# An expert's low part subtracted one item later, and two gathers of routing shares issued three scatters apart

## The chip, the cores and the metric

The kernel runs on one core of a Trainium2 chip. The metric is the device time of one execution in microseconds (us); three executions of a kernel are taken and their median is compared.

## What is computed

1024 tokens of 256 features pass through a linear layer with low-rank adapters (the condition), and the result goes through a mixture of 8 experts, of which each token uses the best 2. The output is the input plus the mixture. Cut to what matters here:

```python
router_logits = xf @ w_gate.T                       # xf: 1024 conditioned tokens
routing_weights = softmax_integer(router_logits)    # fixed-point table of exp
top_w, top_i = jax.lax.top_k(routing_weights, 2)
top_w = top_w / top_w.sum(axis=-1, keepdims=True)
combine = jnp.zeros((T, E)).at[jnp.arange(T)[:, None], top_i].add(top_w)
for e in range(8):
    h = jax.nn.silu(xf @ w1[e].T) * (xf @ w3[e].T)  # 256 -> 704
    out = out + combine[:, e:e + 1] * (h @ w2[e].T) # 704 -> 256
return x + out
```

All inputs and outputs are fp32.

## The kernel before, in words

Only the chosen tokens of an expert are computed. The 2048 choices are sorted by expert into 23 **slots** of 128 rows (SLOTS), every slot belonging to one expert; with these inputs the experts receive 263, 261, 263, 262, 206, 267, 249 and 277 choices, so that the slots of experts 0 to 7 are 3, 3, 3, 3, 2, 3, 2 and 3 in number. A slot is worked off in three **items** (STEPS), each a share of the 704 hidden features, so that the main loop has 69 items; item i is step j = i % 3 of slot s = i // 3.

To keep fp32 accuracy with TensorE's faster formats, every operand is split into a high part (a rounded copy) and a low part (the operand less its high part). Each product is then made of three matmuls.

What each engine does for item i, in its own program order:

- **TensorE**: `gate_up(i)` (L1169, L1178) into one of four PSUM banks `gu`; at one step of each slot the turn of the next slot's rows (L1149); `turn_hidden(i - 1)` (L1185), a transpose of the hidden tile; `down(i - 2)` (L1206 to L1208, and L1200 and L1201 for the last of a slot) into the one PSUM bank `ya`. The first `down` of a slot begins the sum in `ya` anew and so waits for `y_out`, that is until the slot before has been copied out.
- **ScalarE**: `silu(i)` (L611, or L615 and L616 at j = 2), the high part of the next slot's rows (`xs_hi`, L553) and the high part of the hidden tile (`h_hi`, L553).
- **VectorE**: `hidden(i)` (L872, or L877 and L879), the low part of the next slot's rows (L864), `hidden_lo(i - 1)` (L887), and at j = 1 `slot_out(s - 1)` (L893), the copy of `ya` into `rows`, which raises `y_out`. Some further work is put at single items: `SHARED_AT` names the items at which `expert_lo(e, 2)` (L847) stands, the low part of the third piece (1280 columns) of the weights of experts 2 and 3. It raises `third_ready`.
- **GpSimd (POOL)**: makes the rest of the low parts (and from expert 4 on the high parts) of the weights and issues the gathers of the slots' rows in between (L452). For expert 3 it waits for `third_ready` before its last step `tail_low` (L463), which raises `w_ready`; TensorE waits for `w_ready` when it is about to begin an expert. After the last expert POOL scatters each finished slot's rows to HBM (L474): `scatter(s)` waits for `hid_done` to reach s + 44 (PACE), so that there is one scatter per item, and for `y_out`.

The last two slots (DIRECT) aren't scattered but joined by matmuls at the end. They need the routing shares of their rows: VectorE works the shares out at items 47 to 52, ScalarE's queue stores them to HBM (L664) at item 53, and two indirect gathers on POOL's queue (L536), one for each slot, fetch 128 numbers of 4 bytes each into `share`. `SHARES_BEHIND` names the scatter after which they are issued. ScalarE waits for both (`share_in`) at item 67, in `direct_hi`. All weights' transfers are issued by SyncE.

The lines that decide the order around the change:

```python
if j == turned_at(s) and s + 1 < SLOTS:
    slot_lo(s + 1)
...
if 1 <= i <= ITEMS:
    hidden_lo(i - 1)
...
if i in SHARED_AT:
    expert_lo(SHARED_AT[i], 2).then_inc(third_ready, 1)
if i >= 4 and j == 1:
    slot_out(s - 1)
```

Of the kernel before, what the change touches and what calls it, by code (L numbers as in the profile page):

```python
# [60 lines left out]
DIRECT = 2  # L61
# [9 lines left out]

CLEAR = SLOTS - HI_COLS // DIM
FETCHED = {2: (CLEAR, 10), 3: (10, 14), 4: (14, 18), 5: (18, 20), 6: (20, 21), 7: (21, SLOTS)}
SHARED_AT = {8: 2, 13: 3}

# [1 line left out]

SHARES_AT = ITEMS - 22  # L80
SHARE_PARTS = 6
SHARES_BEHIND = 12
STAGED = 1
STAGED_LOW = 3

# [19 lines left out]
def moe_kernel(nc, x_dram, pack_dram, idx_dram, w_dram, wtail_dram, comb_dram, out_dram):  # L105
    c_dram = nc.dram_tensor("cond_rows", (TOKENS, DIM), F32, kind="Internal").ap()
    y_dram = nc.dram_tensor("expert_rows", (TOP * TOKENS + SLOTS * P, DIM), F32, kind="Internal").ap()
    share_dram = nc.dram_tensor("shares", (P * TOP * TILES, 1), F32, kind="Internal").ap()
    with ExitStack() as ctx:
        def sb(name, shape, dt=F32):  # L110
            return ctx.enter_context(nc.sbuf_tensor(name, shape, dt))
# [4 lines left out]
        def sem(name):  # L116
            return ctx.enter_context(nc.semaphore(name))
# [49 lines left out]
        share_at = sb("share_at", [P, DIRECT], U32)  # L167
        share = sb("share", [P, DIRECT])
# [136 lines left out]
        share_in = sem("share_in")  # L305
# [110 lines left out]
        def _(pool):  # L416
# [53 lines left out]
            def scatter(s):  # L470
                pool.wait_ge(dst_ready, 1)
                pool.wait_ge(rows_zeroed, 16)
                pool.wait_ge(y_out, s + 1)
                nc.gpsimd.indirect_dma_start(  # L474
                    out=y_dram[:, :], out_offset=bass.IndirectOffsetOnAxis(ap=dst_i[:, s:s + 1], axis=0),
                    in_=rows[:, s, :], in_offset=None).then_inc(scattered, 16)
# [52 lines left out]
            for s in range(SENT):  # L529
                pool.wait_ge(hid_done, s + PACE)  # L530
                scatter(s)
                if s == SHARES_BEHIND:
                    pool.wait_ge(share_at_ready, 1)
                    pool.wait_ge(share_out, 16 * TOP)
                    for l in range(DIRECT):
                        nc.gpsimd.indirect_dma_start(  # L536
                            out=share[:, l:l + 1], out_offset=None, in_=share_dram[:, :],
                            in_offset=bass.IndirectOffsetOnAxis(ap=share_at[:, l:l + 1], axis=0)).then_inc(share_in, 16)

            pool.wait_ge(pool_step, 4)  # L540
            for l in range(DIRECT):
# [134 lines left out]
        def _(dve):  # L676
# [167 lines left out]
            def expert_lo(e, k):  # L844
                cols = PIECES[k]
                dve.wait_ge(whi_ready, len(PIECES) * e + k + 1)
                return nc.vector.tensor_tensor(lo_part(e, cols), from_raw(e)[:, cols], as_f32(hi_part(e, cols)),  # L847
                                               ALU.subtract)
# [9 lines left out]
            def expert_tail_lo(e):  # L858
                stack = stack_part(e, LOW_HALF)
                return nc.vector.tensor_tensor(stack, raw_tail(e, LOW_HALF), as_f32(stack), ALU.subtract)  # L860
# [89 lines left out]
            for i in range(ITEMS + 2):  # L950
# [21 lines left out]
                if i == 3:  # L972
                    destinations()
                    expert_lo(1, 2)
                    expert_tail_lo(1).then_inc(w_ready, 1)
# [3 lines that stand above are left out]
# [355 lines left out]
```

## Time and profile before

| what | value |
|---|---|
| three executions | 203.08, 204.21 and 204.86 us; median 204.21 us |
| the profiled execution | 204.69 us, of which the span from the first to the last instruction is 203.0 us |
| busy share of the span | TensorE 95%, VectorE 54%, ScalarE 41%, GpSimd 64% |
| TensorE's granted clock | full speed (2.4 GHz) throughout |

The profile is one execution of the program, taken by the hardware profiler. Times in its rows are microseconds from the start of the span; "PE" is TensorE's matmuls, "PEld" its weight loads, "DVE" VectorE, "ACT" ScalarE, "POOL" GpSimd. L847 is line 847 of the kernel. The ends of matmuls are modelled, since they are pipelined; spans on POOL are rough.

### The profile page before, as it was taken

Reading aid. Unit: us, or ns where it says so; the run is one execution under the profiler, and the core shown is the slowest. Engines: PE = TensorE matmul, PEld = TensorE weight load, DVE = VectorE, ACT = ScalarE, POOL = GpSimd, SP = SyncE. Lnnn points to the kernel's source line nnn. Section 1 sums busy time; section 2 is a strip of 40 time slices with the busy share of each in tenths; the row PEclk is TensorE's granted clock in tenths of the full one; section 3 lists DMA queues with packets and bytes.
Section 4 is the critical chain, followed back from the end, with each engine's and each line's share of the span. In section 5 each row is a group of like instructions: output and inputs, shape, how many; then the busy total and the mean of one; then the engine's idle time right before and its main releaser. Section 6 shows DMA issues by size and latency. Waiting matters only on the chain.

```text
span 203.0 us, 3879 instructions
## 1 busy us (share of the span) xinstructions
PE 192.1 (95%) x1209; PEld 169.2 (83%) x1209; DVE 108.7 (54%) x308; ACT 82.4 (41%) x224; POOL 129.7 (64%) x116
## 2 busy tenths in 40 slices
PE   7699999899998999999999999999999997999992
PEld 6387997788897899889988998899888886989881
DVE  0678899783646345334534453444675434435483
ACT  2576583368733143323332343233323323333560
POOL 8300004559899999999999999996345473316700
PEclk9999999999999999999999999999999999999999
DMA  5999320799996115283274383017212111110915
GB/s 134 408 368 361 136 103 19 232 301 385 349 396 235 57 55 155 61 284 75 88 258 126 90 260 113 0 16 275 74 55 53 53 55 61 43 55 26 346 73 208
DMA packets 14403, 32.67 MB, mean 161 GB/s; under 512 B 2384, under 2 KB 7632, under 8 KB 14256
## 3 DMA queue, kind: packets, MB, share of 16 engines
q1 hardware_dynamic: 10704, 25.17, 36.2%
q0 software_dynamic: 2128, 5.64, 8.8%
q10 hardware_dynamic: 1552, 1.61, 2.4%
q8 instruction: 12, 0.20, 0.4%
q14 instruction: 7, 0.06, 0.1%
HBM read 25.45 MB, written 6.96 MB: 160 GB/s over the span
## 4 chain that ended last, share of the span: by engine, by line
PE 80%; DVE 10%; DMA 5%; ACT 2%; issue 1%; SPq 0%; DVEq 0%
PE gu L1169 27%; PE gu L1178 14%; PE ya L1206 8%; PE ht L1185 7%; PE ya L1207 7%; PE ya L1208 6%; DMA x<-x_t 4%; DVE w_all L847 3%; PE xt L1149 2%; PE gu L1223 2%; DMA rows<-cond_rows,src_i 2%; PE ya L1201 1%; PE gu L1055 1%; PE ya L1200 1%; PE gu L1236 1%
## 5 line engine op out<-in xcount | busy, mean ns | idle before, releaser
L1169 PE MATMUL gu<-w_all,xs_hi 128*128 (+2 forms) x276 | 70.9, 378 | 0.1
L872 DVE TENSOR_TENSOR hid<-gu,sg 128x256 f32<-128x256 f32 x46 | 19.5, 425 | 65.8 <-ACT sg L611 62.5
L1169 PEld LDWEIGHTS gu<-w_all,xs_hi 128*128 128x128 f32 x276 | 46.8, 188 | 4.4 <-issue 0.3
L611 ACT ACTIVATE sg<-gu 128x256 f32<-128x256 f32 x46 | 17.7, 384 | 75.3 <-PE gu L1178 75.3
L458 POOL TENSOR_TENSOR w_all<-raw,w_all 128x1024 fp32r<-128x1024 f32 (+2 forms) x14 | 44.0, 3156 | 3.6 <-DVE w_all L860 3.5
L452 POOL DMA_INDIRECT rows<-cond_rows,src_i x22 | 23.6, 1073 | 30.5 <-DVE src_i L828 25.9
L1206 PE MATMUL ya<-w_all,h_hi 128*128 (+1 forms) x115 | 38.4, 334 | 2.4 <-DVE rows L893 2.3
L1178 PE MATMUL gu<-w_all,xs_lo 128*128 (+1 forms) x138 | 40.6, 375 | 0.0
L474 POOL DMA_INDIRECT expert_rows<-rows,dst_i x21 | 20.3, 969 | 26.3 <-DVE hid L872 14.5
L1207 PE MATMUL ya<-w_all,h_hi 128*128 (+1 forms) x115 | 32.5, 282 | 0.0
L1208 PE MATMUL ya<-w_all,h_lo 128*128 (+1 forms) x115 | 32.2, 280 | 0.0
L1178 PEld LDWEIGHTS gu<-w_all,xs_lo 128*128 128x128 f32 x138 | 25.6, 188 | 4.0
L887 DVE TENSOR_TENSOR h_lo<-ht,h_hi 128x256 fp32r<-128x256 f32 x69 | 28.6, 415 | 0.3 <-ACT h_hi L553 0.3
L553 ACT ACTIVATE h_hi<-ht 128x256 fp32r<-128x256 f32 x69 | 26.7, 387 | 0.5 <-PE ht L1185 0.4
L1185 PE MATMUL ht<-ident,hid 128*128 128x128 f32 x138 | 26.3, 272 | 0.3 <-DVE hid L872 0.3
L1206 PEld LDWEIGHTS ya<-w_all,h_hi 128*128 128x128 f32 x115 | 21.7, 188 | 4.6 <-issue 3.7
L1185 PEld LDWEIGHTS ht<-ident,hid 128*128 128x128 f32 x138 | 18.5, 140 | 4.7 <-DVE hid L872 0.6
L1207 PEld LDWEIGHTS ya<-w_all,h_hi 128*128 128x128 f32 x115 | 21.8, 190 | 0.0
L1208 PEld LDWEIGHTS ya<-w_all,h_lo 128*128 128x128 f32 x115 | 21.7, 189 | 0.0
L507 POOL CAST w_all<-raw 128x1024 fp32r<-128x1024 f32 (+2 forms) x12 | 16.8, 1401 | 0.0
L615 ACT ACTIVATE sg<-gu 128x128 f32<-128x128 f32 x23 | 6.4, 279 | 21.9 <-PE gu L1178 19.6
L877 DVE TENSOR_TENSOR hid<-gu,sg 128x128 f32<-128x128 f32 x23 | 6.7, 291 | 12.4 <-ACT sg L616 11.7
(190 smaller groups left out, 261.1 us busy)
## 6 DMA issues: line engine op xcount, KB each, us to landing
raw<-expert_weights SPq DMA_DIRECT2D x6, 896.0 KB
raw<-expert_weights SPq DMA_DIRECT2D x6, 640.0 KB
raw<-expert_weights SPq DMA_DIRECT2D x6, 512.0 KB
expert_rows<-zeros SPq DMA_DIRECT2D x1, 2048.0 KB
rows<-expert_rows SPq DMA_DIRECT2D x4, 512.0 KB, 5.0
cond_rows<-c_rows ACTq DMA_DIRECT2D x4, 256.0 KB, 2.0
raw<-x_t SPq DMA_DIRECT2D x1, 1024.0 KB
out_t<-raw SPq DMA_DIRECT2D x4, 256.0 KB, 2.2
```

The costliest lines, as they stand in the source:

```text
L452: nc.gpsimd.indirect_dma_start(out=rows[:, s, :], out_offset=None, in_=c_dram[:, :], in_offset=bass.IndirectOffsetOnAxis(ap=src_i[:, s:s + ...
L458: return nc.gpsimd.tensor_tensor(lo_part(e, cols), from_raw(e)[:, cols], as_f32(hi_part(e, cols)), ALU.subtract)
L474: nc.gpsimd.indirect_dma_start(out=y_dram[:, :], out_offset=bass.IndirectOffsetOnAxis(ap=dst_i[:, s:s + 1], axis=0), in_=rows[:, s, :], in ...
L553: return nc.scalar.activation(out, in_, ACT.Copy)
L872: nc.vector.tensor_tensor(hid[i % HBUFS][:, :].rearrange("p (a b) -> p a b", b=P), bank[:, :].rearrange("p (a k b) -> p a k b", k=2, b=P)[ ...
L887: nc.vector.tensor_tensor(h_lo[i % HBUFS][:, :], ht[i % 2][:, 0:2 * P], as_f32(h_hi[i % HBUFS][:, :]), ALU.subtract).then_inc(h_lo_ready, 1)
L1169: nc.tensor.matmul(out, stay_hi[:, kc * P:(kc + 1) * P], moving(at, part + first + kc * P, n), start=kc == 0 and part == HI_COLS, stop=False)
L1178: last = nc.tensor.matmul(out, stay_lo[:, kc * P:(kc + 1) * P], moving(at, first + kc * P, n), start=False, stop=kc == KC - 1)
L1185: last = nc.tensor.transpose(ht[i % 2][:, q * P:(q + 1) * P], hid[i % HBUFS][:, q * P:(q + 1) * P], ident[:, :])
L1206: nc.tensor.matmul(out, stay_hi, w_l, start=j == q == 0, stop=False)
L1207: nc.tensor.matmul(out, stay_hi, w_h, start=False, stop=False)
L1208: last = nc.tensor.matmul(out, stay_lo, w_h, start=False, stop=False)
```

## The change

`SHARED_AT` moves expert 3's third piece from item 13 to item 14. Item 13 is step j = 1 of slot 4 and has a `slot_out`, ahead of which the subtraction stood; item 14 is step j = 2 and has none. The second of the two gathers of shares, which stood right behind the first after scatter 12, is now issued after scatter 15. The two waits ahead of a gather stand ahead of each of them.

```diff
-SHARED_AT = {8: 2, 13: 3}
+SHARED_AT = {8: 2, 14: 3}
...
-SHARES_BEHIND = 12
+SHARES_BEHIND = (12, 15)
...
                 scatter(s)
-                if s == SHARES_BEHIND:
+                if s in SHARES_BEHIND:
+                    l = SHARES_BEHIND.index(s)
                     pool.wait_ge(share_at_ready, 1)
                     pool.wait_ge(share_out, 16 * TOP)
-                    for l in range(DIRECT):
-                        nc.gpsimd.indirect_dma_start(
-                            out=share[:, l:l + 1], out_offset=None, in_=share_dram[:, :],
-                            in_offset=bass.IndirectOffsetOnAxis(ap=share_at[:, l:l + 1], axis=0)).then_inc(share_in, 16)
+                    nc.gpsimd.indirect_dma_start(
+                        out=share[:, l:l + 1], out_offset=None, in_=share_dram[:, :],
+                        in_offset=bass.IndirectOffsetOnAxis(ap=share_at[:, l:l + 1], axis=0)).then_inc(share_in, 16)
```

## Rows read from the trace of the kernel before

**Rows 1.** The page, busy time: us, share of the span, instructions.
```profile
PE 192.1 (95%) x1209; PEld 169.2 (83%) x1209; DVE 108.7 (54%) x308; ACT 82.4 (41%) x224; POOL 129.7 (64%) x116
```

**Rows 2.** The chain that ended last: start, us, what.
```profile
64.32 1.40 DVE w_all L847
...
94.63 0.94 PE gu L1169 x4
...
166.41 1.95 PE gu L1178 x2
```

**Rows 3.** Busy time by stretch, slots 3 and 4, cut at each slot's first matmul.
```profile
core 0: us, PE busy (x) PEld busy (x) DVE busy (x) ACT busy (x) POOL busy (x), PEclk, DMA share, GB/s
52.23:59.03 6.80, 6.80 (x45) 6.12 (x44) 4.72 (x13) 3.75 (x11) 6.31 (x5) 1.00 1.12 368
59.03:67.28 8.25, 7.04 (x44) 6.16 (x44) 4.58 (x11) 2.26 (x8) 7.46 (x5) 1.00 0.64 243
```

**Rows 4.** The same view, slots 18 and 19.
```profile
156.33:163.14 6.81, 6.81 (x45) 6.04 (x44) 2.92 (x10) 2.27 (x8) 3.56 (x4) 1.00 0.21 60
163.14:171.43 8.29, 7.23 (x45) 6.10 (x44) 3.17 (x10) 2.26 (x8) 4.76 (x6) 1.00 0.15 50
```

**Rows 5.** All waits of PE: who waited, us in total, times, longest.
```profile
PE ya L1206 <- DVE rows L893: 2.3, 3, 1.2
```

**Rows 6.** Timeline, items 13 and 14: start, us, engine, line; idle time before it.
```profile
62.83 0.38 PE L1185 MATMUL ht<-ident,hid 128*128 128x128 f32 x2
...
64.23 1.48 DVE L847 TENSOR_TENSOR w_all<-raw_low,w_all 128x1280 fp32r<-128x1280 f32 x1
...
64.71 0.38 PE L1185 MATMUL ht<-ident,hid 128*128 128x128 f32 x2
64.83 1.71 POOL L452 DMA_INDIRECT rows<-cond_rows,src_i  x1 [0.30 <-issue]
...
65.63 0.42 DVE L893 COPY rows<-ya 128x256 f32<-128x256 f32 x1
...
66.30 0.38 PE L1206 MATMUL ya<-w_all,h_hi 128*128 x1 [1.21 <-DVE rows L893]
...
67.81 0.75 POOL L463 TENSOR_TENSOR w_all<-raw_low_tail,w_all 64x256 fp32r<-64x256 f32 x1
```

**Rows 7.** Timeline of DVE, items 8 and 9, then 11 and 12.
```profile
52.74 1.48 DVE L847 TENSOR_TENSOR w_all<-raw,w_all 128x1280 fp32r<-128x1280 f32 x1
54.42 0.42 DVE L872 TENSOR_TENSOR hid<-gu,sg 128x256 f32<-128x256 f32 x1 [0.19 <-ACT sg L611]
...
58.89 0.41 DVE L887 TENSOR_TENSOR h_lo<-ht,h_hi 128x256 fp32r<-128x256 f32 x1
60.91 0.42 DVE L872 TENSOR_TENSOR hid<-gu,sg 128x256 f32<-128x256 f32 x1 [1.60 <-ACT sg L611]
```

**Rows 8.** Timeline of POOL from 134 to 172 us.
```profile
140.51 0.96 POOL L474 DMA_INDIRECT expert_rows<-rows,dst_i  x1 [0.34 <-issue]
...
162.47 0.98 POOL L536 DMA_INDIRECT share<-shares,share_at  x1 [0.30 <-issue]
163.75 0.96 POOL L536 DMA_INDIRECT share<-shares,share_at  x1 [0.30 <-issue]
...
166.33 0.98 POOL L474 DMA_INDIRECT expert_rows<-rows,dst_i  x1 [0.31 <-issue]
```

**Rows 9.** Timeline of all engines around item 58.
```profile
160.08 0.38 ACT L611 ACTIVATE sg<-gu 128x256 f32<-128x256 f32 x1 [1.67 <-PE gu L1178]
...
166.25 0.62 PE L1178 MATMUL gu<-w_all,xs_lo 128*128 x2
...
168.38 0.38 ACT L611 ACTIVATE sg<-gu 128x256 f32<-128x256 f32 x1 [2.99 <-PE gu L1178]
```

**Rows 10.** DMA queues, packets: the stretch 158.75 to 159.0, then 166 to 168 us.
```profile
q14 instruction: 1, 0.01, 12.6%
...
q0 software_dynamic: 85, 0.18, 26.1%
```

## The prediction

> **What bounds the kernel now.** I read the page's busy times first: TensorE is busy 95% of the span and VectorE 54% [rows 1], so TensorE sets the end, and a change elsewhere is worth only what TensorE stands idle for it. Next the chain that ended last. It consists of matmuls from item to item, and two places break the pattern: a VectorE piece of 1.40 us at 64.32, which is the subtraction of expert 3's third piece, and a pair of L1178 matmuls credited with 1.95 us at 166.41 [rows 2], where the timeline gives the two matmuls 0.62 [rows 9]. Then the busy times cut at each slot's first matmul: an ordinary slot takes 6.80 or 6.81 us, slot 4 takes 8.25 and slot 19 takes 8.29 [rows 3, 4]. So TensorE loses 1.45 us in one slot and 1.48 us in another. The clock was full in all four stretches. The list of TensorE's waits names VectorE's copy L893 as the greatest releaser, 2.3 us in three waits, the longest 1.2 [rows 5]; the only row of it that names POOL is of a memset at the start, so no weights were late.
>
> The timeline shows the first loss. In item 14 TensorE turned the hidden tile at 64.71 and could have begun the next slot's `down`, but `ya` was not copied out: VectorE had begun the subtraction at 64.23, took 1.48 us, and copied at 65.63; TensorE went on at 66.30 [rows 6]. The second loss starts on another engine: the matmuls of item 58 ended at 166.25 + 0.62 = 166.87, and ScalarE's silu, idle and waiting for nothing else in its program, began only at 168.38, after 2.99 us of idleness where the same step a slot earlier had 1.67 [rows 9]. VectorE's chain and the copy of `ya` came late behind it. What held ScalarE is named nowhere. What lies just ahead are the kernel's only two gathers of 4-byte shares, issued at 162.47 and 163.75, with late scatters behind them [rows 8].
>
> **Part 1: the subtraction an item later.** It takes away the 1.48 us ahead of the copy. The copy then follows the low part of the hidden tile at about 64.23 and ends near 64.65, about when the transposes at 64.71 are issued [rows 6], so the wait goes. The gain is the whole excess of the slot, 8.25 - 6.80 = 1.45 us [rows 3]; the named wait of 1.21 us [rows 6] is the lower bound. I take 1.45, since that is what TensorE's schedule lost.
>
> The same instruction is put back at item 14. There VectorE ends an ordinary j = 2 item with the low part at 58.89 + 0.41 = 59.30 and starts the next product at 60.91, after 1.60 us of idleness [rows 7]; 1.48 us fits with 0.12 to spare. Expert 2's third piece is a precedent at the same step: it started at 52.74 in item 8, took 1.48 us, and the next product still waited 0.19 us for ScalarE [rows 7]; the stretch in which it lies took TensorE 6.80 us [rows 3]. If the cover were gone, the product would be late by the excess, and TensorE turns such a tile at 62.83, that is 1.50 us after the product's end at 60.91 + 0.42 = 61.33 [rows 6, 7]; only what goes beyond that costs. Cost: zero, at most 0.1 us.
>
> POOL waits for this piece ahead of `tail_low`. With the stall gone, slot 5 begins at 59.03 + 6.80 = 65.83, the low part ends some 0.27 us behind that as it did a slot earlier, at 66.1, and the piece ends at about 67.6; POOL reaches `tail_low` at 67.81 today [rows 3, 6, 7]. So it comes just in time; half a microsecond late would do no harm either, since expert 3 begins with slot 9 (the first three experts fill three slots each), whose matmuls start at 94.63 [rows 2]. Behind `tail_low` on POOL stands the conversion of expert 4, needed later still. The gather of rows that lay beside the piece took 1.71 us [rows 6] where the like gathers of scattered rows take 0.96 [rows 8]: the later piece will stretch the next gather instead, and its rows are not wanted for slots.
>
> The piece itself took 1.48 us with a gather beside it and without change from one place to the other [rows 6, 7], so VectorE was not held up by POOL. The Trainium skill (SBUF — State Buffer, "SBUF: two separate sides") says that a VectorE operation with two SBUF inputs and a GpSimd operation that reads SBUF exclude each other, and that whichever starts first keeps the shared ports to its end. By that rule a POOL operation that started first would delay the piece by up to its own length, and with the 0.96 us of a gather the next product would be 0.8 us late, inside the 1.50 us of cover; the sum would be the same by row and by rule.
>
> **Part 2: the gathers apart.** No instruction is added: the two waits ahead of the second gather (the shares stored, their addresses made) were over before the first. Scatter 13 comes 1.28 us earlier (163.75 - 162.47), scatter 16 waits that long behind the second gather; a scatter is released each item, that is each 6.80 / 3 = 2.3 us, so the backlog is gone after one. Scatter 15 is three items behind scatter 12, one slot: with part 1's gain taken off, the first gather goes out at 162.47 - 1.45 = 161.0 and the second 6.8 us later, at 167.8. ScalarE needs it in item 67, nine items or three slots (20 us) after item 58. On these counts the cost is zero. The gain is bounded by the stall: at most 8.29 - 6.81 = 1.48 us [rows 4], at least zero, and below zero if each gather alone brings such a stall, +1.48. I take 1.48: this is the one place where ScalarE is late in the steady loop, and it follows the one pair of gathers. Indirect transfers in quick succession alone don't do it: the scatter at 140.51 was the last of four about 1.3 us apart [rows 8], and the chain shows nothing late there.
>
> **The sum.** 204.69 - 1.45 - 1.48 = 201.76, say 201.8 us. The profiled execution is 0.48 above the median of 204.21; on the median the same sum gives 201.28. The lowest execution, 203.08, is 1.61 below the profiled one, about one stall; so the second loss may not be there in every execution, and then 203.08 - 1.45 = 201.63 is what all would come to. What is late next: nothing as large; the rest of the loop runs at 6.8 us a slot, and the end shifts with it.
>
> **Rivals.**
> *The ScalarE stall stays, once.* Its cause is not shown. If it belongs to the first gather, or to ScalarE's own program at that point, only part 1 counts: 204.69 - 1.45 = 203.24 us, 202.8 on the median. For it: nothing in the trace ties ScalarE to a gather. Against: the place. In the stretch of the stall only the software queue of the gathers and scatters carried packets, 85 of them; the nearest packet of the small instruction queue lies at 158.75 [rows 10], eight microseconds earlier. The Trainium skill (Runtime: NRT & Kernel Launch, "Instruction fetch mechanics") says that each engine fetches its program in blocks through a queue of its own, mostly hidden. By that rule a stall at a block's border would stay with its instruction and give the time of this rival; the trace has no such packet in the stall.
> *Each gather brings its own stall.* Scatter 15 is released by an item of the same step as scatter 12's, one slot later, so the second gather meets ScalarE in the same phase as the first. If each alone holds ScalarE for 1.48 us, two slots lose what one loses now: 204.69 - 1.45 + 1.48 = 204.72 us, slower than before by a trace, by 0.5 us against the median. It decides as soon as one gather's stall exceeds 1.45 us. Against: two gathers 1.28 us apart show one stall today.
> *The subtraction stalls TensorE again.* Were the piece stretched beyond 0.12 + 1.50 us, or the copy of `ya` late for another reason, the first gain is lost and the second stays: 204.69 - 1.48 = 203.21 us.
> *Neither gain comes:* 204.7 us.
>
> **How the numbers follow.** Forecast 0.50; the stall stays 0.30; two stalls 0.08; the first gain lost 0.07; neither 0.05. The forecast's own range is 201.0 to 202.2 (201.28 on the median less 0.3, 201.8 and 0.4 for the spread of executions). With the rivals at 202.8 to 203.24 and 0.4 for the spread, 201.0 to 203.7 holds the time 8 times in 10. One per cent, about what a measurement of this kernel tells from no change, is 2.04 us: faster means below 202.17, slower above 206.25. Faster is the forecast but for its upper edge, 0.44, and 0.03 of the second case: 0.47. Slower is 0.03, the rest 0.50.
>
> **What would show it.** Right: slot 4 at 6.8 us; the copy L893 ahead of L847, and L847 ending before the next product; the longest wait for L893 gone from TensorE's list; POOL's `tail_low` near 67.8; gathers near 161.0 and 167.8; all slots from 16 to 21 at 6.8 to 7.0 us, and no silu later than 0.1 us behind its matmuls. Wrong: a slot of over 8 us behind one gather or both, or a new idle stretch ahead of the product of item 15. The prediction fails if the ScalarE stall is not the gathers' doing.

## The result and the profile after

The changed kernel takes 202.97 us (median of 7 executions, 202.05 to 203.54), the kernel before, run beside it, 204.21 us (7, 203.08 to 204.99). The ratio is 0.9933, 95% interval 0.9905 to 0.996: a gain of 0.7%, less than the one per cent that the prediction counts as faster. The profiled execution of the changed kernel took 203.51 us, with a span of 201.8 us, 1.2 us less than before. The forecast was 201.8, its range 201.0 to 203.7; the time is that of the rival "the ScalarE stall stays, once" (202.8 on the median). Why it came out there is another matter.

Busy times of the changed kernel, cut as [rows 3] and [rows 4] are: slots 3, 4, 18 and 19; then two stretches near the start.

```profile
core 0: us, PE busy (x) PEld busy (x) DVE busy (x) ACT busy (x) POOL busy (x), PEclk, DMA share, GB/s
53.80:60.62 6.82, 6.82 (x45) 6.13 (x44) 4.74 (x13) 3.82 (x11) 5.48 (x6) 1.00 1.10 366
60.62:67.47 6.85, 6.85 (x45) 6.15 (x44) 3.01 (x10) 2.27 (x8) 6.08 (x4) 1.00 0.68 262
...
156.68:163.49 6.81, 6.81 (x44) 6.13 (x44) 2.85 (x10) 2.26 (x8) 3.56 (x4) 1.00 0.21 60
163.49:170.30 6.81, 6.81 (x44) 6.12 (x44) 3.00 (x10) 2.27 (x8) 3.87 (x5) 1.00 0.18 60
...
8.00:10.00 2.00, 1.91 (x7) 1.47 (x8) 1.48 (x6) 0.88 (x2) 0.00 (x0) 0.66 1.06 440
10.00:12.00 2.00, 2.00 (x8) 1.78 (x7) 1.65 (x2) 1.61 (x5) 0.00 (x0) 0.50 0.99 414
```

Both long slots are gone: slot 4 takes 6.85 us where it took 8.25 [rows 3], slot 19 takes 6.81 where it took 8.29 [rows 4]. That is 2.88 us, close to the forecast's 1.45 + 1.48, yet the span fell by only 1.2. The last two lines say where most of the rest went: between 8 and 10 us TensorE was granted 0.66 of its clock in the mean, and between 10 and 12 us 0.50, that is the lower of its two levels, 1.2 GHz. The same stretches of the profile of before had the full clock, 2.4 GHz:

```profile
8.00:10.00 2.00, 1.59 (x10) 1.04 (x8) 1.68 (x6) 0.95 (x1) 0.00 (x0) 1.00 1.03 430
10.00:12.00 2.00, 1.84 (x12) 1.66 (x13) 1.80 (x2) 2.00 (x5) 0.00 (x0) 1.00 0.99 412
```

Set silu beside silu, the two traces differ so. The first silu of the loop starts 1.13 us later in the changed kernel (33.79 against 32.66 us): the clock. At item 6 it is 1.59 later: ScalarE's copy of a piece of weights waited 1.92 us for the piece to land, where before it waited 1.45. At item 15 it is 0.20 later: 1.40 us came back in slot 4. At item 60 it is 1.17 earlier: 1.35 came back in slot 19. So +1.13 + 0.46 - 1.40 - 1.35 = -1.16, which leaves 0.01 of the 1.17 to small shifts in between. Neither of the first two is touched by the change, which begins at item 13. A single pair of profiles could not tell what the change did.

The step of part 1, timeline of the changed kernel, items 13 to 15 (start, us, engine, line, tiles; in brackets the idle time before it and who ended it):

```profile
65.83 0.42 DVE L893 COPY rows<-ya 128x256 f32<-128x256 f32 x1
...
66.49 0.38 PE L1206 MATMUL ya<-w_all,h_hi 128*128 x1
67.06 0.95 POOL L452 DMA_INDIRECT rows<-cond_rows,src_i  x1 [0.30 <-issue]
67.66 1.48 DVE L847 TENSOR_TENSOR w_all<-raw_low,w_all 128x1280 fp32r<-128x1280 f32 x1
69.29 0.73 POOL L463 TENSOR_TENSOR w_all<-raw_low_tail,w_all 64x256 fp32r<-64x256 f32 x1 [1.28 <-DVE w_all L847]
69.32 0.42 DVE L872 TENSOR_TENSOR hid<-gu,sg 128x256 f32<-128x256 f32 x1 [0.18 <-ACT sg L611]
```

The copy now stands ahead of the subtraction, `down` begins at 66.49 without the 1.21 us of waiting of [rows 6], and the subtraction ends at 69.14, before the product at 69.32. In the list of TensorE's waits the longest for that copy is 0.3 us in place of 1.2 [rows 5]:

```profile
PE ya L1206 <- DVE rows L893: 0.3, 1, 0.3
```

Around item 58, POOL's gathers of shares and ScalarE's silus of items 58 and 60 in the changed kernel:

```profile
162.80 0.98 POOL L536 DMA_INDIRECT share<-shares,share_at  x1 [0.30 <-issue]
167.24 0.38 ACT L611 ACTIVATE sg<-gu 128x256 f32<-128x256 f32 x1 [1.67 <-PE gu L1178]
169.62 0.97 POOL L536 DMA_INDIRECT share<-shares,share_at  x1 [0.31 <-issue]
171.72 0.38 ACT L611 ACTIVATE sg<-gu 128x256 f32<-128x256 f32 x1 [1.72 <-PE gu L1178]
```

The gathers stand 6.82 us apart, and no silu is late: 1.67 us of idleness where [rows 9] had 2.99. The profile looks as the forecast wanted it. Whether the gathers had anything to do with it had to be tried.

### The profile page after: what moved, and what is told of

Read it like the earlier page. It is cut to its first block, busy times and chain, and to the rows that moved or that the text cites. A ratio compares the mean times of both kernels' runs of the same rounds, so it can differ in the third digit from the quotient of the medians.

```text
span 201.8 us, 3880 instructions
## 1 busy us (share of the span) xinstructions
PE 193.5 (96%) x1209; PEld 170.7 (85%) x1209; DVE 108.6 (54%) x308; ACT 82.5 (41%) x224; POOL 127.7 (63%) x116
## 3 DMA queue, kind: packets, MB, share of 16 engines
q10 hardware_dynamic: 1552, 1.61, 2.5%
## 4 chain that ended last, share of the span: by engine, by line
PE 83%; DVE 8%; DMA 5%; ACT 1%; issue 1%; DVEq 0%; SPq 0%
PE gu L1169 27%; PE gu L1178 14%; PE ya L1206 8%; PE ht L1185 7%; PE ya L1207 7%; PE ya L1208 7%; DMA x<-x_t 3%; PE xt L1149 2%; DVE w_all L847 2%; PE gu L1223 2%; DMA rows<-cond_rows,src_i 2%; PE ya L1201 1%; PE ya L1200 1%; PE gu L1055 1%; PE gu L1236 1%
## 5 line engine op out<-in xcount | busy, mean ns | idle before, releaser
L452 POOL DMA_INDIRECT rows<-cond_rows,src_i x22 | 21.9, 994 | 31.6 <-DVE src_i L828 27.1
```

The lines of the kernel that those rows point to most:

```text
L452: nc.gpsimd.indirect_dma_start(out=rows[:, s, :], out_offset=None, in_=c_dram[:, :], in_offset=bass.IndirectOffsetOnAxis(ap=src_i[:, s:s + ...
```

## The experiments

Theory A, the prediction's: the subtraction and the pair of gathers each cost about 1.45 us in every execution. Theory B, its rival: part 1 alone brings the gain, and the late silu belongs to something else, chance included. The lines above leave both open.

**Each part alone.** e1 is the kernel before with part 1 only, e2 with part 2 only.

```diff
-SHARED_AT = {8: 2, 13: 3}
+SHARED_AT = {8: 2, 14: 3}
```


> Part 1 alone: the third piece of expert 3 at item 14, both gathers behind scatter 12 as before. Theory A (the two gathers in quick succession hold ScalarE for 1.5 us in most executions): slot 4 takes 6.8 us, but a silu some 3 to 5 us behind the second gather begins 1.3 to 1.5 us late; the median is about 1.4 us above that of the changed kernel, 204.2 to 204.4 us. Theory B (the late silu is a rare event that the gathers don't cause, so that part 1 is the whole gain): no late silu behind the gathers, and the median is that of the changed kernel, 203.0 us, ratio to before 0.993.

```diff
-SHARES_BEHIND = 12
+SHARES_BEHIND = (12, 15)
...
-                    for l in range(DIRECT):
-                        nc.gpsimd.indirect_dma_start(
+                    nc.gpsimd.indirect_dma_start(
```


> Part 2 alone: the second gather behind scatter 15, the third piece at item 13 as before. Slot 4 keeps its 8.25 us under every theory. Theory A: no late silu, the median 1.4 us under before, ratio 0.993, 202.8 us. Theory B: the median is that of before, ratio 1.000 within 0.003, 204.2 us.

Measured: e1 203.07 us (12 executions), ratio 0.9945 (0.9919 to 0.9971), a gain of 1.12 us (0.59 to 1.66) against 204.45. e2 203.86 us (12), ratio 0.9987 (0.9960 to 1.0015), a gain of 0.27 us (-0.31 to 0.82). The interval of e2 leaves out 1.48 us. In e1's profile no silu is late, though its two gathers follow each other as before; the gathers and the silu of item 58 in e1:

```profile
161.25 0.98 POOL L536 DMA_INDIRECT share<-shares,share_at  x1 [0.30 <-issue]
162.53 0.96 POOL L536 DMA_INDIRECT share<-shares,share_at  x1 [0.30 <-issue]
165.70 0.39 ACT L611 ACTIVATE sg<-gu 128x256 f32<-128x256 f32 x1 [1.67 <-PE gu L1178]
```

So A's second half, a cost in every execution, falls.

**The pair elsewhere, and more pairs.** e3 keeps the gathers together and moves them four scatters on, with part 1. If the pair held ScalarE, the late silu would move with it. e4 adds to part 1 four further pairs behind scatters 13 to 16, into a tile that nothing reads (work added, none left out); SyncE waits for them at the end.

```diff
-SHARES_BEHIND = 12
+SHARES_BEHIND = 16
```


> Part 1 with the pair of gathers, still back to back, four scatters later (behind scatter 16). Theory A: the late silu goes with the pair, to some 3 to 5 us behind 171 to 173 us, and costs 1.3 to 1.5 us there (less if it falls on a step with more slack); about 204.3 us. Theory B: no late silu tied to the pair, 203.0 us. If the late silu stays at item 58, it belongs to ScalarE's own program.

```diff
+MORE = (13, 14, 15, 16)
...
+                if s in MORE:
+                    for l in range(DIRECT):
+                        at = MORE.index(s) * DIRECT + l
+                        nc.gpsimd.indirect_dma_start(
+                            out=share_more[:, at:at + 1], out_offset=None, in_=share_dram[:, :],
...
+            sp.wait_ge(more_in, 16 * DIRECT * len(MORE))
```


> Part 1 with the pair behind scatter 12 and the same two gathers repeated, into a scratch tile, behind scatters 13 to 16: five pairs, ten gathers. Theory A: up to five late silus of 1.5 us each, a median 3 to 7 us above the kernel with one pair. Theory C (each gather costs on its own): the same or more. Theory B: POOL's backlog of scatters grows by some 8 us and is gone before the last scatter; no late silu, 203.0 us.

Measured: e3 202.85 us (10), ratio 0.9923 (0.9891 to 0.9955). e4 203.69 us (10), ratio 0.9985 (0.9956 to 1.0013), about 0.6 us above e1's median; among executions of like clock it is 1.25 us (below). Timeline of e4, the last added pair and the silu behind it (its lines stand ten lower):

```profile
172.73 0.96 POOL L546 DMA_INDIRECT share_more<-shares,share_at  x1 [0.30 <-issue]
173.99 0.94 POOL L546 DMA_INDIRECT share_more<-shares,share_at  x1 [0.30 <-issue]
177.07 0.39 ACT L621 ACTIVATE sg<-gu 128x256 f32<-128x256 f32 x1 [1.75 <-PE gu L1188]
```

Five pairs, and no silu is late behind one; in e3 none either, with the pair at 170.78 and 172.07. What e4's profile lost against e1's, 0.9 us, lies at the end: from its last silu to the end of the span 13.21 us where e1 has 12.33. POOL is later with its own last steps, since eight gathers at 1.26 us stand ahead of them, and TensorE's last stage waits for POOL:

```profile
PE gu L1233 <- POOL w_all L552: 0.4, 1, 0.4
```

Each of these programs has one profile, so a stall that the pairs bring in few executions would not show; five in every execution, 3 us or more, are ruled out by the times.

**The kernel before again.** If the late silu belongs to the program, it comes in each execution. Three more profiles of the kernel before, unchanged.

> The kernel before once more, for its profile: does the late silu of item 58 come again? Theory A (the two gathers bring it): yes, in most looks, at the item 3 to 5 us behind the second gather. Theory B (an event by chance, not tied to the gathers): in few looks or none, or at another item; the other slots 6.8 us, slot 4 at 8.25 us each time.

> As the first look. Theory A: the late silu again. Theory B: not, or elsewhere; slot 4 at 8.25 us.

> As the first look. Theory A: the late silu again. Theory B: not, or elsewhere; slot 4 at 8.25 us.

Measured: 204.70, 203.82 and 203.60 us. Busy times of the first of them, slots 4 and 19:

```profile
60.49:68.74 8.25, 7.04 (x44) 6.16 (x44) 4.59 (x11) 2.27 (x8) 7.46 (x5) 1.00 0.63 234
...
164.63:171.44 6.81, 6.81 (x44) 6.17 (x44) 2.98 (x10) 2.27 (x8) 4.17 (x5) 1.00 0.18 60
```

Slot 4 is as long as in [rows 3], slot 19 is an ordinary slot. The silu of item 15 comes 3.81, 3.82 and 3.82 us after that of item 14 in the three, 3.80 in the first profile, 2.40 in e1. No silu is late in any of the three. Of all 14 profiles of this study one has it, the very one that the prediction was made from; of the 12 whose gathers follow each other, one.

**What part 1 rests on.** e5 leaves the subtraction at item 13 and only swaps the two `if` blocks, so that the copy comes first: if the order alone is the cure, the later item isn't needed.

```diff
-                if i in SHARED_AT:
-                    expert_lo(SHARED_AT[i], 2).then_inc(third_ready, 1)
                 if i >= 4 and j == 1:
                     slot_out(s - 1)
+                if i in SHARED_AT:
+                    expert_lo(SHARED_AT[i], 2).then_inc(third_ready, 1)
```


> Only the order is changed: the third piece stays at item 13 but stands behind the copy of the slot's rows; the gathers as before. Theory of part 1 (the cost is the wait of TensorE for the copy, not the subtraction): the copy starts 1.4 us earlier and slot 4 takes 6.8 us. The product of item 14, whose VectorE idle time is 0.68 us in ordinary slots, comes some 0.7 us late, but TensorE needs it 1.3 us after its ordinary end, so that nothing is lost: ratio 0.993, 203.1 us. Rival (VectorE's room in an item decides, and an item of step 1 has too little): slot 4 keeps 0.5 to 0.8 us of its excess, ratio 0.997.

e6 and e7 load item 14 further, with part 1: one and two subtractions of 1024 columns into space that is free there, ahead of the piece (work added, none left out). They measure the cover that the prediction counted as 0.12 us of idleness and 1.50 us until TensorE turns the tile.

```diff
+                if i == 14:
+                    spare_out = hot_r[:, :, :].rearrange("p a b -> p (a b)").bitcast(F32)
+                    for _ in range(1):
+                        chain(nc.vector.tensor_tensor(spare_out, raw_low[:, DOWN_AT:DOWN_AT + HALF * 2],
...
```


> Part 1 with one extra subtraction of 1024 columns (some 1.2 us, written to a tile that nothing reads any more) ahead of the third piece at item 14. If the cover is as the prediction said (0.12 us of VectorE's idle time and then TensorE's 1.3 to 1.5 us before it needs the late product and low part), the product of item 15 is late by 1.1 to 1.2 us and TensorE loses nothing: slot 5 begins on time and the median is that of part 1, 203.1 us. If VectorE's 1.60 us are the whole cover, TensorE loses 1.1 us and the median is 204.2 us.

> The same with two extra subtractions: 3.9 us of work against 1.60 us of idle time, the product late by 2.3 to 2.4 us. With the further cover of 1.3 to 1.5 us TensorE loses 0.8 to 1.1 us (204.0 us); without it 2.3 us (205.4 us).

Measured: e5 202.30 us (7), ratio 0.9914 (0.9883 to 0.9946). e6 202.27 us (9), ratio 0.9904 (0.9878 to 0.993). e7 203.72 us (10), ratio 0.9973 (0.9944 to 1.0001). Timeline of e5:

```profile
64.15 0.41 DVE L893 COPY rows<-ya 128x256 f32<-128x256 f32 x1
64.48 1.48 DVE L847 TENSOR_TENSOR w_all<-raw_low,w_all 128x1280 fp32r<-128x1280 f32 x1
64.71 2.08 POOL L452 DMA_INDIRECT rows<-cond_rows,src_i  x1 [0.30 <-issue]
65.89 0.28 DVE L877 TENSOR_TENSOR hid<-gu,sg 128x128 f32<-128x128 f32 x1
67.03 0.38 PE L1185 MATMUL ht<-ident,hid 128*128 128x128 f32 x2
```

The next product stands right behind the piece and TensorE turns it on time. Timeline of e7:

```profile
66.22 2.53 DVE L979 TENSOR_TENSOR hot_r<-raw_low,w_all 128x1024 f32<-128x1024 f32 x2
68.79 1.49 DVE L847 TENSOR_TENSOR w_all<-raw_low,w_all 128x1280 fp32r<-128x1280 f32 x1
70.20 0.42 DVE L872 TENSOR_TENSOR hid<-gu,sg 128x256 f32<-128x256 f32 x1
70.67 0.44 PE L1191 MATMUL ht<-ident,hid 128*128 128x128 f32 x2 [0.71 <-DVE hid L872]
71.09 0.38 PE L1212 MATMUL ya<-w_all,h_hi 128*128 x1
```

The same product, turn and `down` of item 15 in e1:

```profile
67.89 0.43 DVE L872 TENSOR_TENSOR hid<-gu,sg 128x256 f32<-128x256 f32 x1 [0.17 <-ACT sg L611]
69.80 0.38 PE L1185 MATMUL ht<-ident,hid 128*128 128x128 f32 x2
69.94 0.36 PE L1206 MATMUL ya<-w_all,h_hi 128*128 x1
```

In e6 the added 1.27 us make the product 1.15 us late (69.04 against 67.89 in e1, 0.09 of it already there at item 14) and TensorE loses nothing; in e7 2.53 us are too many and TensorE waits (the silu of item 17 comes 3.25 us after that of item 16 in e7, 2.09 in e1). The cover lies between 1.27 and 2.53 us; counted as 0.12 + 1.50 = 1.62 it asks for a loss of 2.53 - 1.62 = 0.91 in e7, and the intervals show 3.25 - 2.09 = 1.16. Measured from the silu of item 14 (65.06 in e7, 65.08 in e1) the turn itself came 0.89 late, as counted; a further 0.28 went behind it, since `down` began 0.42 after the turn in e7 and 0.14 in e1.

**The start.** e8 is part 1 with two more of the matmuls on zeros that TensorE runs while the first data arrive; e9 is part 1 with ScalarE's last piece of expert 2 an item later, so that ScalarE doesn't stand before the silus waiting for weights to land.

```diff
-WARM_UP = 11
+WARM_UP = 13
```


> Part 1 with 13 instead of 11 warm-up matmuls at the start. In the changed kernel's profile TensorE's granted clock fell to half between 8.4 and 12.2 us and the first silu came 1.1 us later than in the profile of before. If the idle stretch ahead of the first real matmul brings the fall, two more matmuls fill it: no profile shows it, and the median falls by 0.2 to 0.4 us against part 1, to 202.7 us. If it is chance of the transfers' landing, the median stays at 203.0 us or rises by the 0.3 us by which the warm-up reaches into the first matmul.

```diff
-                if 3 <= i < 6:
+                if 3 <= i < 5:
...
+                if i == 6:
+                    expert_hi(2, 2)
+                if 7 <= i < 10:
...
-                    expert_hi(3, i - 6)
+                    expert_hi(3, i - 7)
```


> Part 1, and on ScalarE the high part of expert 2's third piece at item 6 instead of 5, with expert 3's three pieces an item later each. In every profile so far that copy waited 0.7 to 2.4 us for the last weights of expert 2 to land, with silu 6 queued behind it, so that items 5 to 8 took 7.3 to 8.4 us instead of 6.8. If that wait is TensorE's loss, silu 6 comes on time and the median falls by 0.5 to 1.2 us under part 1, to 202.0 to 202.5 us, ratio 0.989 to 0.992. If something else is late there (the second copy, or the shares of VectorE's work that follow it), the median stays at 203.0 us.

Measured: e8 202.64 us (6), ratio 0.9917 (0.9885 to 0.9949), with the full clock from 8 to 12 us in its profile. e9 202.54 us (6), ratio 0.9924 (0.9894 to 0.9954). Timeline of e9: the copy no longer waits for its landing, and the silu of that item starts ahead of it:

```profile
47.58 0.39 ACT L611 ACTIVATE sg<-gu 128x256 f32<-128x256 f32 x1 [2.01 <-PE gu L1180]
...
48.13 1.49 ACT L553 ACTIVATE w_all<-raw 128x1536 fp32r<-128x1536 f32 x1
```

But items 5 to 10 took 11.85 us where they took 12.13 in e1, 0.28 less, and the profiles without this edit lie between 11.72 (e3) and 12.70 (e2), so that this shows nothing. The start of e9's profile was slow as well: its first silu came at 33.25 (32.51 in e1) although the granted clock reads 1.00. Timeline of e9, two of the first matmuls:

```profile
7.87 0.79 PE L1013 MATMUL ht<-x_hi,pk_hi 128*128 128x512 f32 x1
8.46 0.63 PE L1016 MATMUL ht<-x_hi,pk_lo 128*128 128x512 f32 x1
```

In e1 these two took 0.50 and 0.40; 0.77 and 0.63 is what the changed kernel's took where its clock read 0.50. Neither e8 nor e9 can be told from part 1 alone, and none of the versions beats the changed kernel by more than these intervals.

**The clock, by execution.** Each execution has a mean granted clock, and it falls in two groups, 0.988 to 0.992 and 0.996 to 1.0, with none between. Three of the 14 profiles are of the lower group (the changed kernel, e3, the first further one of before), and in all three the clock fell between 8 and 12 us; they lost 0.87 to 1.13 us up to the first silu against the first profile of before. The mean doesn't show every slow start: e9's profile, 0.59 us late by the same measure, has a mean of 1.000. For the executions without a profile the fall at the start is inferred from the mean. This sorting was made after the runs; two executions of before at over 1000 us are left out.

| kernel | upper group: median us (n) | lower group: median us (n) |
|---|---|---|
| before, beside the experiments | 203.97 (43) | 204.84 (27) |
| part 1, shares anywhere (changed kernel, e1, e3) | 202.45 (17) | 203.45 (12) |
| e2, part 2 alone | 203.85 (11) | 205.12 (1) |
| e7 | 203.48 (7) | 204.28 (3) |

At like clocks part 1 brings 1.52 and 1.39 us and part 2 alone 0.12. The table pools executions of several chips. On the chip of e1 to e4 alone, part 1 (e1, e3) brings 203.91 - 202.33 = 1.58 us in the upper group and 204.94 - 203.32 = 1.62 in the lower, part 2 brings 203.91 - 203.85 = 0.06, and e4 loses 203.58 - 202.33 = 1.25 against part 1, of which its profile shows 0.88 at the end. On the chip of e5 to e8, e7 loses 203.48 - 202.27 = 1.21 against e6, close to the 1.16 of the traces. e1's 1.12 us comes from its ratio; the two medians differ by 1.38. e5, e6 and e8 have none of the lower group in 22 executions, which flatters their ratios: e5's and e6's 202.30 and 202.27 stand beside 202.45. The kernel before had 10 of 23 in it on that chip, a difference that is hardly chance; what decides the share is not shown.

## Why the prediction was right in its range and wrong in one term

**Part 1 was right, in mechanism and size.** Forecast 1.45 us; slot 4 fell by 1.40 in the traces and the executions at like clocks by 1.39 to 1.62. e5 shows that the order behind the copy is what counts, not the later item.

**Its cover was right.** The product waited 0.18 us for ScalarE behind the piece (forecast: 0.12 to spare), `tail_low` came at 69.29, that is 67.69 when the 1.60 us by which this execution was late is taken off (forecast 67.8), e6 and e7 put the limit between 1.27 and 2.53 us, and in e7 the turn came 0.89 us late where 0.12 + 1.50 us of cover ask for 0.91. The 0.28 us that TensorE lost behind the late turn wasn't in the count.

**"The later piece will stretch the next gather instead" was wrong, and cost nothing.** In the changed kernel the gather was over (67.06 + 0.95 = 68.01) 1.13 us before the piece was, at its usual length. In e5 the gather issued 0.23 us into the piece took 2.08 us in place of 0.95 to 0.97, and the piece kept its 1.48. Which began first decided for the gather: in the changed kernel the gather began, in e5 and in [rows 6] the piece. The Trainium skill (SBUF — State Buffer, "SBUF: two separate sides") says that whichever of the two starts first has the shared ports to its end, and e5 agrees. The other direction doesn't: in the changed kernel the gather had 0.35 us to go when the piece began, in e1 it began 0.04 us ahead of it, and the piece took 1.48 and 1.49 us all the same. Here VectorE held the gather up and the gather didn't hold VectorE up, so the delay of up to 0.96 us that the prediction reckoned by that rule didn't come. The same page of the Trainium skill (SBUF — State Buffer, "A bandwidth-pool intuition that's wrong (but worth ruling out)") puts the end of such a block about 0.115 us behind VectorE's end; no row shows when the gather of e5 went on, and its own end came 0.83 us behind the piece. Timeline of e1:

```profile
66.20 0.95 POOL L452 DMA_INDIRECT rows<-cond_rows,src_i  x1 [0.30 <-issue]
66.24 1.49 DVE L847 TENSOR_TENSOR w_all<-raw_low,w_all 128x1280 fp32r<-128x1280 f32 x1
```

**"I take 1.48" for part 2 was wrong.** This is the step that failed. It took the late silu for a cost of every execution and laid it on what stood just ahead of it. Apart, the gathers brought 0.27 us (-0.31 to 0.82); together, moved, and five times over (e1, e3, e4) they brought no late silu; and the unchanged kernel didn't show it in three further profiles. So the forecast counted a stall of one execution as one of the kernel. The lower bound named beside it, zero, was the value to take. It also took the stall off the median (201.28), in which it mostly wasn't. That the time lies in the stated range is owed to the room left for a rival: the forecast's own part of the range, 201.0 to 202.2, missed.

**The rival gave the number, not the reason.** "The ScalarE stall stays, once" came to 202.8, and 202.97 was measured. But the stall didn't stay with the program: it is in neither the changed kernel's profile nor the further profiles of before. The rule cited for it (the Trainium skill, Runtime: NRT & Kernel Launch, "Instruction fetch mechanics") would bind a stall to its place in the program, and the three further profiles of the same program have none there. In those three, the first profile of before, the changed kernel and e1 alike, each of the two instruction queues has a packet ahead of this place, one 5 to 6 us and one at most 2 us before the silu of item 57 (in the first profile the second lies between 162.7 and 163.7 us, nearer than the prediction saw); only one of the six has the late silu. On the median this comes to the same: what is seldom there can't be taken away.

**The hint in the spread was read, but not followed to its end.** The prediction saw that the fastest execution of before was 1.61 us below the profiled one and thought of the late silu. For that execution this was right: its clock was full, and without the 1.35 us of the late silu its 204.69 would be 203.34, 0.26 above the fastest. The step left out is that a stall which is missing from the fastest may be missing from most, and then little of it can be won on the median. In general the spread has other sources: the two clock groups of before lie 0.87 us apart, and within the upper group alone the times run from 203.26 to 205.39. The weights that land ahead of silu 6 probably have a share in that: ScalarE's copy waited 0.7 to 2.4 us for them in the 13 profiles without e9's edit.

What held ScalarE for 1.35 us in that one execution stays open: it was seen once and never again, and no run could ask it.

## What to carry to other kernels

Price a stall only when it is in a second profile of the same program, or when its releaser is named: here the one with a named releaser (VectorE's copy) came back in every profile of before to 0.02 us, the one without a name never. Side work on an engine that also frees the bottleneck's buffer belongs behind the freeing instruction, and its cover is that engine's idle time plus the time until the bottleneck needs the next result. Where a kernel's executions fall in two groups by granted clock, compare within a group before believing half a per cent.

## What the runs showed of the hardware that was not expected

The clock of one and the same program fell in some executions and not in others: in one of the four profiles of the kernel before and, by the mean clock, in 27 of 70 further executions. Ahead of the fall TensorE had stood idle for its first inputs; timeline of the changed kernel, two of those waits:

```profile
6.65 0.50 PE L1011 MATMUL ht<-x_hi,pk_hi 128*128 128x512 f32 x1 [0.88 <-ACT x_hi L553]
...
8.09 0.51 PE L1011 MATMUL ht<-x_hi,pk_hi 128*128 128x512 f32 x1 [0.71 <-ACT x_hi L553]
```

In the profile of before the same two waits took 1.16 and 0.24 us and the clock stayed up. The waits alone don't sort the profiles: e2 waited 1.42 and 0.65 us and stayed up, the first further profile of before waited 1.23 and 0.25 and fell. Whether the longer warm-up of e8 keeps it up isn't settled: none of its 6 executions is of the lower group, but of the 16 of e5 and e6, without it, none is either.

An indirect gather of 128 numbers of 4 bytes held POOL as long (0.94 to 0.98 us, with 0.30 before it) as one of 128 rows (0.95 us).

VectorE's subtraction of 1280 columns and a gather of rows on POOL met in every profile, and the hold went one way. A gather issued 0.04 to 1.12 us after the subtraction began ended 0.81 to 0.83 us after the subtraction's end, in all 16 such cases of the 14 profiles: wherever it was issued, about 0.82 us of its usual 0.95 was still to be done. Where the gather began first and was still under way (19 cases), the subtraction kept its 1.48 or 1.49 us. Where VectorE began only 0.01 to 0.02 us ahead (e4, and e6 and e7 with the added subtraction), the gather took its usual 0.95 us; e4's subtraction took 1.55.
